# Another order in the first half of a main sequence, and the first product of the inverses in 24 tiles

## The reference

```
h  = x + attn(layernorm(x))          # attn: two residual steps of its own
     y  = layernorm(.)*g + b ;  q, k, v = split(y @ gates_w + gates_b) ; lr = y @ lr_w + lr_b
     k  = k / |k| ;  K = tril(k k^T, -1) ;  u = solve(K + I, v) ;  out = ((q k^T) (lr * u)) @ out_w + out_b
     then + relu(layernorm(.) @ w1 + b1) @ w2 + b2
out = h + (silu(n @ w_gate^T) * (n @ w_up^T)) @ w_down^T,   n = layernorm(h),  integer weights / 127
```

## Time and profile before

| | us |
|---|---|
| median of three runs | 1578.6 (1577.91 to 1579.26) |
| the profiled execution, its own time | 1577.6 |
| its span, from the first to the last instruction | 1575.9 |
| TensorE busy | 1538.7 (98%) |
| VectorE busy | 1182.4 (75%) |
| ACT and POOL busy | 794.5 and 781.2 (50% each) |
| mean TensorE clock | 0.998 |

### The profile page before, as it was taken

One profiled execution on the slowest core, in us unless ns is written; L12 is line 12 of the kernel. 1 busy time (PEld: TensorE's weight loads), 2 busy tenths in 40 slices (PEclk: granted clock), 3 DMA queues, 4 the chain that ended last, 5 costly groups with the idle time before them and its releaser, 6 DMA issues.

```text
span 1575.9 us, 30053 instructions
## 1 busy us (share of the span) xinstructions
PE 1538.7 (98%) x10694; PEld 1354.9 (86%) x10694; DVE 1182.4 (75%) x3103; ACT 794.5 (50%) x1600; POOL 781.2 (50%) x918
## 2 busy tenths in 40 slices
PE   8999998899999999999999999999999999999998
PEld 7999997788888888888888888888888888888887
DVE  6767874578887777888877778888877777777774
ACT  6878774354444444444444444444444444444442
POOL 5456872244444554444445544444444444444442
PEclk9999999999999999999999999999999999999999
DMA  7999997112222322222222222222222222222200
GB/s 241 340 311 314 327 330 247 61 61 74 75 74 75 114 74 75 74 75 74 74 75 98 91 74 74 70 67 72 73 94 82 75 74 74 75 74 74 69 20 27
DMA packets 150166, 178.20 MB, mean 113 GB/s; under 512 B 78850, under 2 KB 132098, under 8 KB 141826
## 3 DMA queue, kind: packets, MB, share of 16 engines
q1 hardware_dynamic: 150018, 176.28, 34.0%
HBM read 98.64 MB, written 77.59 MB: 112 GB/s over the span
## 4 chain that ended last, share of the span: by engine, by line
PE 60%; DVE 15%; ACT 4%; POOL 3%; issue 2%; ACTq 0%; DVEq 0%; POOLq 0%
PE ps L175 31%; PE ps L1102 15%; PE ps L1112 5%; PE ps L1033 4%; DVE xinv L1408 3%; DVE bs L1602 3%; DVE xh2T_lo L1463 2%; PE ps L1008 2%; ACT work L1319 2%; POOL sc L1620 2%; DVE a L1597 2%; DVE late L1488 1%; DVE gl_hi L1513 1%; ACT hh L1284 1%; PE ps L1022 1%
## 5 line engine op out<-in xcount | busy, mean ns | idle before, releaser
L1674 POOL TENSOR_TENSOR hl<-late,hh 128x512 fp32r<-128x512 f32 x128 | 165.6, 1294 | 206.0 <-ACT hh L1284 206.0
L1279 ACT ACTIVATE late<-ps 128x512 f32<-128x512 f32 x192 | 114.5, 596 | 170.4 <-PE ps L1102 170.4
L1112 PE MATMUL ps<-wdT,hh 128*128 128x256 f32 x744 | 197.7, 303 | 0.0
L1458 DVE TENSOR_TENSOR late<-ps,late 128x512 f32<-128x512 f32 x192 | 132.7, 691 | 84.9 <-PE ps L1102 83.1
L1288 ACT ACTIVATE z_hi<-ps 128x256 fp32r<-128x256 f32 x128 | 49.2, 384 | 290.7 <-PE ps L1033 290.2
L1112 PE MATMUL ps<-wdT,hl 128*128 128x256 f32 x744 | 181.2, 281 | 0.3 <-DVE hl L1463 0.3
L1284 ACT ACTIVATE hh<-late 128x512 fp32r<-128x512 f32 x192 | 120.8, 629 | 108.9 <-DVE late L1458 108.9
L1620 POOL TENSOR_TENSOR sc<-ls,mhalf 128x4 f32<-128x4 f32 x64 | 65.1, 1018 | 194.5 <-DVE ls L1425 194.5
L1102 PE MATMUL ps<-xh3T_hi,wgT 128*128 128x512 f32 x384 | 153.6, 400 | 1.1 <-DVE xh3T_lo L1463 1.1
L1102 PE MATMUL ps<-xh3T_lo,wuT 128*128 128x512 f32 x384 | 152.2, 396 | 0.0
L1102 PE MATMUL ps<-xh3T_lo,wgT 128*128 128x512 f32 x384 | 152.0, 396 | 0.0
(11 more groups left out here) (216 smaller groups left out, 4703.0 us busy)
## 6 DMA issues: line engine op xcount, KB each, us to landing
xhT_scratch<-xhTk SPq DMA_DIRECT2D x32, 1024.0 KB, 6.2
xhT<-xhT_scratch SPq DMA_DIRECT2D x32, 1024.0 KB, 6.4
gg_scratch<-late SPq DMA_DIRECT2D x32, 640.0 KB, 4.1
gg<-gg_scratch SPq DMA_DIRECT2D x32, 640.0 KB, 3.9
xk<-in_L_attn_x_dram SPq DMA_DIRECT2D x32, 512.0 KB, 5.4
xt<-in_L_attn_x_dram SPq DMA_DIRECT2D x32, 512.0 KB, 4.1
out_dram<-late SPq DMA_DIRECT2D x31, 512.0 KB, 2.9
low_scratch<-late SPq DMA_DIRECT2D x128, 16.0 KB, 2.7
```

What stands on the lines that cost most here:

```text
L1112: mm = pe.matmul(ps[:, (FG, FU)[j // 2], (j % 2) * C:(j % 2 + 1) * C], part[:, h, blk(j)], wdT[:, h, :], start=(h == 0 and part is hh), st ...
L1279: act.activation(sg[:, h % 2, :], ps[:, FG, :], ACT.Silu, scale=QUANT).then_inc(sg_ev[h], 1)
L1458: dve.tensor_tensor(hf[:, h % 2, :], ps[:, up_bank(h), :], sg[:, h % 2, :], ALU.mult).then_inc(hf_ev[h], 1)
L1674: pool.tensor_tensor(hl[:, h, :], hf[:, h % 2, :], hh[:, h, :].bitcast(F32), ALU.subtract).then_inc(hl_ev[h], 1)
```

## The change

The first product is 24 products now: for each block `j` and each pair a < b of 32x32 blocks one product of 32 rows, 32 columns and a contraction over 32, in the tile of the array at rows b and columns a. The banks are A0, A1 and A2 for b = 1, 2, 3, so the product waits for all four evictions of the previous sequence from A0 and A2 (`a0_ev[3]` instead of `a0_ev[1]`) and for `m2_sum` (A1). VectorE writes `p1` with three scalings by -1 instead of the one masked multiply; `upper` and its set-up are gone.

The order changes as follows. TensorE: row block 1 stands behind the first transposes; the last hidden block of `pe_down(3)` stands behind `bt` 2, ahead of `z` 0; in the bodies 0 and 1 all row blocks come earlier, and body 1 gets 34 products of ones. First `xn`: POOL makes block 0, VectorE block 1 (ahead of everything else in its body), ACT blocks 2 and 3 as before. Second `xn`: VectorE makes blocks 0 and 1, ACT blocks 2 and 3, for which VectorE computes the shift. `xhm_hi` moves from VectorE to ACT. VectorE's `gl_hi` moves behind the copy of row block 2, `dve_out(0)` behind `w` 2, one block of `x2` behind `w` 1, `dve_out(1)` behind `z` 0, and the steps of `dve_invert` to other places. POOL makes `gl_lo` after `xa2`.

```diff
-                def pe_level(pe, bank, lhs, rhs, c0, w, rows, done):
+
+                def pe_above(pe):
 
                     for j in range(TB):
-                        mm = pe.matmul(ps[rows, bank, j * w:(j + 1) * w], lhs(j)[:, rows], rhs[:, j, c0:c0 + w], start=True, stop=True)
-                    mm.then_inc(done, 1)
-
-
-                def pe_row_block(pe, bank, f, done):
-
+                        for b in range(1, QPB):
+                            for a in range(b):
+                                mm = pe.matmul(ps[sub(a), above_bank(b), j * SUB:(j + 1) * SUB], diag(j)[sub(b), sub(a)],
+                                               xT32[sub(b), j, sub(b)], start=True, stop=True)
+                                if j == TB - 1:
+                                    mm.then_inc(pT_ps, 1)
...
+                def pe_row_block(pe, i, f):
+
+                    pe.wait_ge((pT_ev, xa_ev, xb_ev)[f - 1], i + 1)
+                    if f == 1:
+                        after(pe, m2_sum, i)
...
-                        mm = pe.matmul(ps[j * SUB:(j + 1) * SUB, bank, 0:f * SUB], p1[:, j, rows], xinv[:, j, 0:f * SUB],
-                                       start=True, stop=True)
-                        mm.then_inc(done, 1)
+                        mm = pe.matmul(ps[j * SUB:(j + 1) * SUB, row_bank(f), 0:f * SUB], p1[:, j, rows],
+                                       xinv[:, j, 0:f * SUB], start=True, stop=True)
+                        mm.then_inc((xa_ps, xb_ps, x128_ps)[f - 1], 1)
...
                     if att:
                         wait(pe, inv_in, i * 32 * QPB)
                         wait(pe, gg_in, i * 16)
-                        after(pe, a0_ev[1], i)
-                        pe_level(pe, A0, diag, xT32, SUB, REST, slice(0, REST), pT_ps)
+                        after(pe, a0_ev[TB - 1], i)
+                        after(pe, m2_sum, i)
+                        pe_above(pe)
                         pe_weights(pe, i, 0)
                     if down:
                         after(pe, sg_ev[HB - 1], i - 1)
                         pe_down(pe, i, 0, range(HB - 1))
-                    if att:
-                        pe.wait_ge(pT_ev, i + 1)
-                        after(pe, m2_sum, i)
-                        pe_row_block(pe, A1, 1, xa_ps)
+                    if att and not down:
+                        if i == 1:
+                            keep_busy(pe, S0, 21)
+                        pe_row_block(pe, i, 1)
                         pe_weights(pe, i, 1)
-                    if mlp:
+                        if i == 1:
+                            keep_busy(pe, S0, 7)
+                        pe_row_block(pe, i, 2)
+                        pe_weights(pe, i, 2)
+                        if i == 1:
+                            keep_busy(pe, S0, 6)
+                    if mlp:
+                        pe.wait_ge(xh2_first, i)
                         pe.wait_ge(xh2_done, i)
                         pe.wait_ge(xh2_rest, i)
                         for k in range(CB):
                             after(pe, x3h_ev[k], i - 1)
                             after(pe, x3l_ev[k], i - 1)
                         pe_transposes(pe, (FO0, FO1), xn, t2_ps)
+                    if att and down:
+                        pe_row_block(pe, i, 1)
                     if down:
                         pe_down(pe, i, 0, (HB - 1,))
                         pe_down(pe, i, 1)
-                    if att:
-                        pe.wait_ge(xa_ev, i + 1)
-                        pe_row_block(pe, A0, 2, xb_ps)
-                        pe_weights(pe, i, 2)
+                    if att and down:
+                        pe_row_block(pe, i, 2)
+                    if att and not down:
+                        pe_row_block(pe, i, 3)
+                        pe_weights(pe, i, 3)
                     if mlp:
                         after(pe, hf_ev[HB - 2], i - 1)
                         pe_mlp1(pe, i, 0)
-                    if att:
-                        pe.wait_ge(xb_ev, i + 1)
-                        pe_row_block(pe, A1, 3, x128_ps)
-                        pe_weights(pe, i, 3)
+                    if att and down:
+                        pe_row_block(pe, i, 3)
...
                     if down:
-                        pe_down(pe, i, 3)
+                        pe_down(pe, i, 3, range(HB - 1))
                     if att:
                         pe_wstep(pe, i, 0)
                         pe_bt(pe, i, 2)
+                    if down:
+                        pe_down(pe, i, 3, (HB - 1,))
+                    if att:
                         pe_zstep(pe, i, 0)
                         pe_weights(pe, i, 7)
                     if mlp:
                         if not att:
                             keep_busy(pe, A0, 18)
                         pe.wait_ge(xh3_done, i)
+                        pe.wait_ge(xh3_rest, i)
...
                     if att:
+                        act.wait_ge(xhm_done, TB * (i + 1))
+                        after(act, bt_ps, i)
+                        act.activation(xhm2[0][:, :, :], xh[:, :, :], ACT.Copy).then_inc(xhm_hi, 1)
                         act_z(act, i, 2)
                         act_weights(act, i, (5,))
                         act_z(act, i, 1)
                         act_weights(act, i, (6,))
+                    if mlp:
+                        act.wait_ge(ln3_shift, i)
+                        for k in range(CB):
+                            act.wait_ge(t2_ps[k], i)
+                        for j in range(2, TB):
+                            act.wait_ge(x2_ev[j], i)
+                            op = act.activation(xn[:, j, :], x2s[i % 2][:, j, :], ACT.Identity,
+                                                scale=sc3[:, 0, j:j + 1], bias=sc3[:, 1, j:j + 1])
+                        op.then_inc(xh3_rest, 1)
+                    if att:
...
-                def masked(dve, i):
-                    dve.wait_ge(pT_ps, i + 1)
-                    dve.tensor_tensor(p1[0:REST, :, SUB:P], levels(A0, REST, slice(0, REST)),
-                                      upper[0:REST, SUB:P].unsqueeze(1).broadcast_to([REST, TB, REST]), ALU.mult).then_inc(pT_ev, 1)
-
-                def row_block(dve, bank, f, src_ps, done, i):
+                def minus_above(dve, i):
+                    dve.wait_ge(pT_ps, TILES * (i + 1))
+                    for b in range(1, QPB):
+                        op = dve.tensor_scalar(p1[0:b * SUB, :, sub(b)],
+                                               ps[0:b * SUB, above_bank(b), 0:TB * SUB].rearrange("p (j c) -> p j c", c=SUB),
+                                               -1.0, None, ALU.mult)
+                    op.then_inc(pT_ev, 1)
...
+                def row_block(dve, i, f):
+                    src_ps, done = ((xa_ps, xa_ev), (xb_ps, xb_ev), (x128_ps, x128_ev))[f - 1]
...
-                def dve_x2(dve, i, half):
+                def dve_x2(dve, i, half, *rows):
...
-                    for j in (2 * half, 2 * half + 1):
+                    for j in rows or (2 * half, 2 * half + 1):
...
                 def dve_body(dve, i, att, mlp, down, m, r):
-                    if att:
-                        masked(dve, i)
+                    if mlp:
+                        dve.wait_ge(l2[2], i)
+                        for k in range(CB):
+                            after(dve, t3_ps[k], i - 1)
+                        dve.tensor_scalar(xn[:, 1, :], a0[:, 1, :], mv2[:, 1, 0:1], sc2[:, 0, 1:2],
+                                          ALU.subtract, ALU.mult).then_inc(xh2_first, 1)
+                    if att:
+                        minus_above(dve, i)
                     if down:
                         dve_hl(dve, i - 1, HB - 1)
                     if att:
+                        row_block(dve, i, 1)
+                        if not down:
+                            row_block(dve, i, 2)
+                    if mlp:
+                        dve_lo(dve, xh2T2[1], xh2T2[0], (FO0, FO1), t2_hi, t2_ev, i)
+                    if att:
+                        if down:
+                            row_block(dve, i, 2)
                         wait(dve, gg_in, i * 16)
                         after(dve, w_ps[0], i)
                         dve.tensor_copy(gl2[0][:, :], gg[:, 0:OFF]).then_inc(gl_hi, 1)
-                        row_block(dve, A1, 1, xa_ps, xa_ev, i)
-                    if mlp:
-                        dve_lo(dve, xh2T2[1], xh2T2[0], (FO0, FO1), t2_hi, t2_ev, i)
+                        row_block(dve, i, 3)
+                    if mlp:
+                        dve_h1_lo(dve, i, 0)
+                    dve_invert(dve, m, r, 0, 1)
+                    if att:
+                        dve_z(dve, i, 3)
+                    if mlp:
+                        dve_h1_lo(dve, i, 1)
+                    if att:
+                        dve_w(dve, i, 2)
                     if down:
                         dve_out(dve, i, 0)
-                    if att:
```

(54 more changed lines are left out.)

27 lines of the change are left out of this document (15 added, 12 removed).

## The result

The changed kernel takes 1632.9 us (median of 4 runs, 1630.9 to 1634.6), the one before 1578.4 on the same chip: a ratio of 1.034, 95% interval 1.033 to 1.036. It is 54.5 us slower, where I forecast 5 us faster, and 32 us above the end of the range. The profiled execution took 1634.6 (span 1632.9).

The account below looks back on a forecast made before the run. TensorE's work plus small holes, about 1 us of 39.8 per sequence, was taken as the bound. Later sequences 6.9 and the end 0.4 less 2.3 in the second sequence gave 5.0 us less, 1573.6 against 1578.6; range 1564 to 1601.

Parts of the forecast that it names:

- tile products and first transposes: Start of a later sequence: tile block 0.03 us dearer, transposes no longer wait, +0.14 after the late hl 5 pass.
- third row block: Third row block of a later sequence: waits no longer, as VectorE copies the second one before dve_out, +0.31 us.
- token product and `z` 1: First token product and z product of block 1: holes of 0.08 and 0.19 us close, +0.27.
- wait at `w` 0: At pe_wstep(0): TensorE comes earlier while VectorE's z_ev[1] comes later, a new wait, -0.45 us with the late weight load.
- second transposes: After w 0: two pe_down passes and the split xn fill the 0.24 us until z 0, +0.24.
- gate products (no inversion step): First gate product: new wait because dve_out(1) stands between z 0 and the x3l subtractions, -0.12 us without an inversion step.
- Second sequence: 34 products of ones fill TensorE's idle time and delay the transposes; some 0.2 us comes back, -2.3 in all.
- First sequence: The first sequence was left at 0 change, within 0.5 us.
- Rival 1: Tile block: tile rows in one column group run one after another, +0.87 us in 30 sequences, 1600; chance 0.20.
- a floor under each start: Part of rival 1: a floor per start, showing only in a long run of small products; chance 0.03 within its 0.20.
- Rival 2: VectorE's new order is later than counted at w 0 and the gate, 0.3 us more each, about 1581; chance 0.12.
- Rival 3: The two new waits don't arise, VectorE's small instructions running closer, and tiles stay cheap: 1560 us; chance 0.08.

Follow-up runs that it names:

- two different edits: Changed kernel with POOL's xa2 addition waiting for the sixth hl of the sequence before, 1590.6 us; changed kernel with that addition in four pieces, 1591.1 us.
- the kernel with POOL's wait: Changed kernel with one wait more, POOL starting the addition xa2 only after hl 5 of the sequence before: 1590.6 us, 1.0067 of before.
- the mended order: Changed kernel with POOL's wait for hl 5, inversion steps behind x3l, dve_out(1) ahead of z 0, no products of ones: 1564.4 us; without tiles 1564.0.

## Why the prediction was wrong, step by step

**The step that failed** is that POOL's new order was costed at nothing. The prediction counts VectorE's new place for `hl` 5 ("ready only 3.0 to 3.4 after the start"; 3.07 where POOL was held back) and prices the late pass at 0.07. It never follows POOL: that `gl_lo`, with its wait for a VectorE cast, no longer stands ahead of `xa2`, so that an addition of 2.4 us moves from 5.4 to 1.7 us after the start and under `hl` 5. Measured, `hl` 5 was out 4.66 us after the start (888.67 + 2.26 - 886.27), and the wait for it is 35.1 us in the trace. Taking only that away gave 42 us of the 54.5, by two different edits, and putting only POOL's order into the old kernel cost 68.

The 42 are more than the 35.1 of that wait, because a wait is counted from the end of the pass before it: from start to start the two passes are 1.55 apart (889.44 to 890.99) and 0.22 where POOL waits, the step behind them is 0.22 instead of 0.12, and some thirty times 1.43 is the 42. What is left against before, 12.8 us between the profiled executions, is 2.5 in the first sequence, 2.5 in the second and 8.2 in the 29 behind them, where those with steps are longer by 0.5 each and those without are shorter by 0.1.

The row that should have warned me was in the trace of before: an inversion step of VectorE took 0.83 instead of 0.40 while POOL's addition ran (VectorE, then POOL):

```profile
422.66 0.83 DVE L208 TENSOR_TENSOR tmp<-low,inv 128x240 f32<-128x240 f32 x1
```

```profile
420.83 2.39 POOL L1651 TENSOR_TENSOR work<-xa,a 128x1024 f32<-128x1024 f32 x1
```

I took such durations as they stood, without asking which instruction of POOL lay beside them. The Trainium skill (SBUF — State Buffer, "Who interferes with whom") says the same in advance: VectorE and GpSimd share a pair of ports as an exclusive lock, an operation of VectorE with two SBUF inputs contends with one of GpSimd that reads SBUF, and "Issue order, not op shape, decides who blocks." The traces agree, with 2.26 against 0.68 where POOL was first and 1.23 against 0.76 where VectorE was. It speaks against this change and is the rule that the prediction should have weighed.

**The terms of a later sequence**, sequence 15 of the kernel with POOL's wait against sequence 15 of before, so that the new cause is out:

| term | forecast | measured |
|---|---|---|
| tile products and first transposes | +0.11 | +0.01 |
| third row block | +0.31 | +0.27 |
| token product and `z` 1 | +0.27 | +0.10 |
| wait at `w` 0 | -0.45 | -0.15 |
| second transposes | +0.24 | +0.14 |
| gate products (no inversion step) | -0.12 | -0.23 |
| sum | +0.36 | +0.14 |

Each is the difference of two starts on TensorE's timeline, before and then with POOL's wait. Counted from the first product they are 3.28 and 3.17 at the first down pass behind row block 1, 7.23 and 6.85 at row block 3, 16.10 and 15.62 at `z` 1, 18.06 and 17.49 at `w` 0 (two passes, 0.24, moved behind it), 20.52 and 20.05 at the transposes, 39.57 and 39.33 at the last up product. That last up product lies 0.23 ahead of the next sequence's first product before, and 0.33 in every kernel with tiles, so the terms are counted from there and not from the first product. The tile block as a whole is then 0.33 + 0.55 for 0.23 + 0.62, 0.03 dearer, just as forecast; what is missing of the first term lies behind it, where I had counted a gain of 0.14 between the first down pass and the one behind row block 1 and the starts give 0.04 (2.66 and 2.62). Up to the second transposes the sum is 0.37 for 0.48: three gains were smaller and the first one is all but gone, and the wait at `w` 0, smaller too, makes up for part of it. I had found the queue at the gate (`z` 0, `dve_out(1)`, `x3l`) and summed it to exactly TensorE's need; it costs 0.23 instead of 0.12, 0.20 of it inside the first four gate products (2.07 instead of 1.87), which wait for the second `x3l`. In sequences with inversion steps it is worse: forecast +0.13 with full ones, measured 40.48 against 40.01, so -0.47. The step there was priced at 0.40 and took 0.89 behind POOL's `xa` addition, the same cause again.

**The rest.** Second sequence: forecast -2.3, measured -2.5 (45.95 for 43.43). First sequence: forecast 0 within 0.5, measured -2.4 (32.15 for 29.76). In the one trace of each of the seven kernels with tiles it takes 32.0 to 32.6, and the clock is at its half level for 6.8 us of it; in the three without tiles (29.8 twice, and 30.9 with the mended order) it is at 1.00 throughout. But the fall isn't in every execution of a kernel with tiles: one run of the changed kernel, with a span of 1629.1 us, has a mean clock of 1.000, where 6.8 us at 0.5 would make it 0.998. Whether the tile products have a part in it is open. The idle time of 0.3 to 0.5 that I expected before `w` 0's product in each sequence isn't there: TensorE's list has two waits on `z_lo`, 2.6 us, in the whole trace.

**The rivals.** Rival 1 (tile rows run one after another) is out: the 48 passes took 0.62, and tiles alone changed the time by 0.1%. The sign that I named, the 24 products over 0.9, did not come, and I was wrong all the same. The part of it that was a floor under each start is out too: 48 passes in 0.55 are 0.011 each. The Trainium skill's floor of about 25 ns (TensorE: Matmul & The Clock Gate, "Back-to-back issue gap") isn't seen between these tiles, and the measurement decides. Rival 2 (VectorE later than counted) had the right engine and direction, and 1581 as its price; it missed the cause, POOL, and so 50 us. Rival 3, two waits that don't arise because VectorE's instructions run closer, is out for this kernel (1633). The mended order comes near its number, 1564 for 1560, by edits that it doesn't have, and its own sum, 1578.6 - 17 - 5, is 1557. No rival had two engines that shut each other out.

## What to carry to other kernels

When an instruction of one engine moves in its queue, ask what the next ones will now run beside, not only what they wait for: a POOL instruction that was held back by a wait may have been the reason that VectorE ran freely. An instruction that takes much longer than its twins, with no idle time before it, was held inside; look for the long instruction of the other engine that ends just before it. Mend it by order (a wait on the short critical one) or by cutting the long one into pieces, and check a change of order and a change of operations as two kernels: here the first held nearly the whole loss and, mended, the whole gain.

## What the runs showed that I had not expected

- POOL and VectorE shut each other out of SBUF for a whole instruction, both ways. The victim's record shows a long duration, not a wait: subtraction 0.68 to 2.26 and cast 0.56 to 2.75 on VectorE, addition 2.39 to 2.91 on POOL. Operations of VectorE with an operand in PSUM are not touched: the three scalings take 0.66 under the addition, and in the kernel with POOL's wait the two subtractions `xh2T_lo` take 0.69 each under it, and 0.69 where they don't meet it.
- Cutting POOL's addition from one of 2.39 into four (0.76, 1.23, 0.73 and 0.73; 3.35 in all, with `hl` 5 in between) won 41.8 us without a wait.
- Products in 32x32 tiles run side by side across tile rows as well as columns: 48 passes of six tiles in 0.62, where eight passes of 96 columns take 0.84.
- With POOL's new order alone in the old kernel, TensorE's clock fell to half nine times, for 3.4 us each, always 5 to 9 us after a sequence's start, behind the hole of up to 1.7 us that `hl` 5 or the cast leaves.
